# A sort in 16-bit pairs, with two self products between sort and counts, in a graph network kernel

## The reference, cut to what matters

```python
xr = jnp.einsum('nd,rde->rne', x, W_rel)            # 3 relations
msg = xr[edge_type, edge_src] + b_rel[edge_type]
agg = jax.ops.segment_sum(msg, edge_dst, num_segments=N_NODES)
xs = jnp.einsum('nd,tde->tne', x, W_self)           # 3 node types
h_self = xs[node_type, jnp.arange(N_NODES)] + b_self[node_type]
return jax.nn.relu(h_self + agg)
```

## Time and profile before

| | |
|---|---|
| median of 3 runs | 872.49 us (870.45 to 872.97) |
| the profiled execution's own time | 873.43 us |
| its span on the core | 871.7 us |
| mean granted TensorE clock | 0.965 |
| share of the span: TensorE, VectorE, ScalarE, GpSimd busy | 90%, 80%, 62%, 33% |

### The profile page before, as it was taken

The page is one execution under the profiler, slowest core; times in us unless marked ns, Lnnn a source line. Parts: engine busy times, 40 slices in busy tenths (PEclk is TensorE's granted clock), DMA queues, the critical chain, the costliest instruction groups (busy, mean ns, idle before and its releaser), DMA issues.

```text
span 871.7 us, 12030 instructions
## 1 busy us (share of the span) xinstructions
PE 785.7 (90%) x3566; PEld 600.5 (69%) x3566; DVE 698.3 (80%) x1253; ACT 542.8 (62%) x1034; POOL 284.5 (33%) x230
## 2 busy tenths in 40 slices
PE   2979799899789889988998999999999999999895
PEld 2657565477467668766777877786777867778674
DVE  7999856799966968887898788977889878997635
ACT  2298213566563422646897678877788677864646
POOL 3000387777300000016760068400863028710000
PEclk9989999999989999998999999999999999999998
DMA  5423246788472340416993199822996249942001
GB/s 118 119 69 104 72 135 191 222 255 253 144 262 95 109 132 1 130 64 169 221 228 115 36 228 225 210 91 79 230 228 158 86 126 211 233 103 69 26 6 54
DMA packets 61330, 122.12 MB, mean 140 GB/s; under 512 B 9097, under 2 KB 22699, under 8 KB 61270
## 3 DMA queue, kind: packets, MB, share of 16 engines
q0 software_dynamic: 22096, 52.18, 27.1%
q1 hardware_dynamic: 39173, 69.17, 25.2%
HBM read 105.60 MB, written 15.73 MB: 139 GB/s over the span
## 4 chain that ended last, share of the span: by engine, by line
PE 60%; DVE 22%; ACT 11%; DMA 4%; issue 3%; POOL 0%; SPq 0%; ACTq 0%; DVEq 0%; POOLq 0%
PE ps L712 12%; PE ps L1046 10%; PE ps L1030 7%; PE ps L1085 7%; PE ps L1070 6%; DVE z_parts L1962 5%; PE ps L820 4%; PE ps L965 3%; PE ps L911 3%; DVE gathered_parts L1709 2%; DVE w L1469 2%; PE ps L704 2%; ACT slot_recs L1149 2%; ACT queued L1301 2%; PE ps L849 2%
## 5 line engine op out<-in xcount | busy, mean ns | idle before, releaser
L680 POOL DMA_INDIRECT queued<-node_rows,srci x92 | 145.5, 1581 | 192.3 <-DMA node_rows<-work 152.9
L1046 PE MATMUL ps<-z_parts,onehot_dst 128*125 128x512 f32 x664 | 190.7, 399 | 2.8 <-DVE z_parts L1962 1.6
L712 PE MATMUL ps<-w,xT 128*125 128x512 f32 x660 | 169.9, 410 | 4.2 <-DVE w L1469 3.1
L1962 DVE SCALAR_TENSOR_TENSOR z_parts<-ps,z_parts 128x512 fp32r<-128x512 f32 x216 | 146.4, 689 | 27.4 <-ACT z_parts L1361 22.4
L1361 ACT ACTIVATE z_parts<-ps 128x512 fp32r<-128x512 f32 x216 | 128.1, 597 | 45.4 <-PE ps L1030 36.9
L712 PEld LDWEIGHTS ps<-w,xT 128*125 128x125 f32 x660 | 125.7, 194 | 35.7 <-issue 5.5
L1046 PEld LDWEIGHTS ps<-z_parts,onehot_dst 128*125 128x125 f32 x664 | 120.3, 186 | 42.4 <-issue 15.0
L1030 PE MATMUL ps<-x_parts,gather_lhs 128*128 x408 | 129.1, 398 | 0.5 <-DVE z_parts L1962 0.5
L1030 PEld LDWEIGHTS ps<-x_parts,gather_lhs 128*128 128x128 f32 x408 | 76.4, 188 | 19.9 <-issue 2.5
L1962 DVE SCALAR_TENSOR_TENSOR z_parts<-queued,z_parts 128x512 fp32r<-128x512 f32 x116 | 79.6, 686 | 7.2 <-ACT z_parts L1361 6.8
L674 POOL DMA_INDIRECT gathered<-rel_rows,rowi x75 | 77.8, 1038 | 22.9 <-issue 21.3
(11 more groups left out here) (285 smaller groups left out, 1125.0 us busy)
## 6 DMA issues: line engine op xcount, KB each, us to landing
w_stage<-in_weights SPq DMA_DIRECT2D x88, 256.0 KB, 3.8
onehot_dst<-onehot_rows SPq DMA_DIRECT2D x80, 250.0 KB, 5.2
onehot_rows<-onehot_dst SPq DMA_DIRECT2D x20, 250.0 KB, 2.4
gather_lhs<-edge_src_rows SPq DMA_DIRECT2D x8, 432.0 KB, 8.3
node_rows<-work SPq DMA_DIRECT2D x20, 160.0 KB, 1.9
queued<-node_rows,srci POOLq DMA_INDIRECT x116, 6.6
node_rows<-work SPq DMA_DIRECT2D x20, 90.0 KB, 2.0
rel_rows<-rel_rows_out SPq DMA_DIRECT2D x10, 160.0 KB, 1.9
```

The costliest lines, as they stand in the source:

```text
L680: gp.indirect_dma_start(Q[k % QR][:, :], None, xb_d, row, compute_op=ALU.add)\
L712: mm = pe.matmul(ps[0:R, bank, :], lt[:, a, k, n * R:(n + 1) * R], w[:, b, k, :], start=first and k == 0 and (a, b) == THREE[0], stop=last ...
L1046: mm = pe.matmul(psf[0:R, bass.ds(d, D)], S[:, j // SK % SR, j % SK, :], Z[:, g % ZR, a, :], start=False, stop=False, skip_group_check=True)
L1962: v.scalar_tensor_tensor(out=Z[:, g % ZR, LO, :], in0=of, scalar=0.0, in1=Z[:, g % ZR, HI, :].bitcast(F32), op0=ALU.max, op1=ALU.subtract) ...
```

## The change

Six edits, all in the first 150 us:

1. The sort's one-hots and products become 16-bit numbers (bf16, and f16 for the record values), laid out as `[pair of columns, value, 2]`, so that the innermost dimension has two neighbours and a step of one in every operand. TensorE reads each column at a step of two. The record values and the weights no longer share a type, so a slot column takes two matmuls, of 166 and of 249 columns, where it took one of 332.
2. The edge weight is kept as three bf16 parts in place of two. VectorE makes the first two parts' products in six of the eight groups (`VEC_W`), and the first part's in the other two; ScalarE makes the rest.
3. The count one-hots compare f16 copies of the records (`slh`, `dlh`) with an f16 pair table (`iota2`) in the same layout.
4. Two transposes of x and the split of the first weights move ahead of VectorE's rank chain, and the bias rows are loaded before the weights.
5. `w_lows(3)` and `w_highs(3)` move from the counts to the end of the sort. Two of the five node tiles of the first self product (the blocks in `SEQ` order, 1 and 2) are made before the counts, in banks 6 and 5, one ahead of the record transposes and one behind them; the other three go among the counts, a piece at each fifth tile from tile 18 on.
6. The first three groups of message one-hots are made before VectorE waits for the counts.

```diff
-VEC_W = (3, 5, 7)
+VEC_W = (0, 2, 3, 4, 6, 7)
-FIRST_FILL, FILL_STEP = 20, 3
+FIRST_FILL, FILL_STEP = 18, 5
+SEQ = (1, 2, 3, 4, 0)
+EARLY = 2
+SBANK = (6, 5, 7, 7, 7)
...
-        OHL = at(l_at, 0, "slot_low", [EP, 2, SG, P], F32R)
-        EQ = at(l_at, 10240, "slot_high", [EP, 2, SG, TE])
-        RH = [at(l_at, 16896 + 13312 * i, f"slot_recs{i}", [EP, SG, NREC, TE], F32R) for i in range(2)]
+        OHL = at(l_at, 0, "slot_low", [EP, 2, SG // 2, P, 2], BF16)
+        EQ = at(l_at, 10240, "slot_high", [EP, 2, SG // 2, TE, 2], BF16)
+        RV = [at(l_at, 16896 + 3328 * i, f"slot_values{i}", [EP, SG // 2, 2, TE, 2], F16) for i in range(2)]
+        RWT = [at(l_at, 23552 + 4992 * i, f"slot_weights{i}", [EP, SG // 2, 3, TE, 2], BF16) for i in range(2)]
...
+            pe.wait_ge(x_in, 16 * len(ROWS))
+            for n in range(2):
+                transposes(n, B[0:R, n, :])
             pe.wait_ge(tot_made, 1)
...
+                if g == 0:
+                    zeros(7)
                 for c in range(SG):
-                    mm = pe.matmul(ps[:, 7, 0:NREC * TE], OHL[:, g % 2, c, :],
-                                   RH[g % 2][:, c, :, :].rearrange("p a t -> p (a t)"),
-                                   start=g == 0 and c == 0, stop=g == NSG - 1 and c == SG - 1)
+                    pe.matmul(ps[:, 7, 0:2 * TE], OHL[:, g % 2, c // 2, :, c % 2], RV[g % 2][:, c // 2, :, :, c % 2],
+                              start=False, stop=False, skip_group_check=True)
+                    mm = pe.matmul(ps[:, 7, 2 * TE:5 * TE], OHL[:, g % 2, c // 2, :, c % 2],
+                                   RWT[g % 2][:, c // 2, :, :, c % 2], start=False, stop=False, skip_group_check=True)
...
+            pe.wait_ge(words_made, 1)
+            for j in range(KT):
+                fill(j)
+            pe.wait_ge(rec_made, 1)
+            pe.transpose(ps[0:TF, 7, 0:P], slf[:, 0:TF], ident[:, :])
+            pe.transpose(ps[0:TF, 7, P:2 * P], wt[:, 0:TF], ident[:, :]).then_inc(rec_tr, 1)
+            pe.wait_ge(yb_out, NREL * NT)
+            for b in range(3):
+                zeros(b)
+            for j in range(KT, 2 * KT):
+                fill(j)
+            pe.wait_ge(typ_out, 1)
+            for b in (3, 4):
+                zeros(b)
+            for b in (6, 5):
+                pe.wait_ge(self_out, SBANK.index(b) + 1)
+                zeros(b)
...
-                for a in ((LO,) if g in VEC_W else (HI, LO)):
+                for a in ((2,) if g in VEC_W else (1, 2)):
                     for c in range(SG):
...
+            self_first(0)
             act.wait_ge(rec_tr, 1)
             nc.scalar.copy(tr_sl[:, :], ps[0:TF, 7, 0:P])
             nc.scalar.copy(tr_w[:, HI, :], ps[0:TF, 7, P:2 * P]).then_inc(rec_rows, 1)
-            act.wait_ge(y_done, NREL * NT)
-            w_highs(3)
...
+            v.wait_ge(rows_hi, 1)
+            v.tensor_tensor(RWL, RW, RWH.bitcast(F32), ALU.subtract).then_inc(rows_split, 1)
+            for n in range(2):
+                tr_low(n, XT, n, n + 1)
+            w_lows(0)
             v.scalar_tensor_tensor(out=loc[:, :, :], in0=blk[:, :, :], scalar=-float(R), in1=ids[:, :, :],
...
+                for a in ((0, 1) if g in VEC_W else (0,)):
+                    v.tensor_tensor(RWT[g % 2][:, :, a, :, :], EQ[:, g % 2, :, :, :],
+                                    per_slot(wbits[:, a, :], g, TE), ALU.mult)
                 for i in range(2):
-                    ins = v.tensor_tensor(RH[g % 2][:, :, i, :], EQ[:, g % 2, :, :],
-                                          val[:, i, c].unsqueeze(2).broadcast_to([EP, SG, TE]), ALU.mult)
+                    ins = v.tensor_tensor(RV[g % 2][:, :, i, :, :], EQ[:, g % 2, :, :, :],
+                                          per_slot(val[:, i, :], g, TE), ALU.mult)
...
+            w_lows(3)
             v.wait_ge(so_used, NSG)
...
+                for to, of in ((SS, slh), (SD, dlh)):
+                    ins = v.tensor_tensor(to[:, g % 2, :, :, :], local_ids(CG), per_tile(of, g * CG, CG), ALU.is_equal)
                 ins.then_inc(cnt_made, 1)
...
+            for g in range(1, SR):
+                onehots(g)
             v.wait_ge(c_done, 1)
```

More of the change, by code:

```diff
@@ L173, in build @@
         bk = early("bk", [EP, EC])
-        val = early("record_values", [EP, 2, EC])
-        wparts = early("weight_parts", [EP, 2, EC], F32R)
+        val = early("record_values", [EP, 2, EC], F16)
+        wparts = early("weight_parts", [EP, 3, EC])
+        wbits = early("weight_parts_b", [EP, 3, EC], BF16)
         slot = early("slot", [EP, EC])
         ti = early("ti", [EP, 2, EC], I32)
-        lohi = early("lohi", [EP, 2, EC])
+        lohi = early("lohi", [EP, 2, EC], F16)
         tri = early("tri", [EP, P])
@@ L753, in _ @@
             pe.matmul(ps[:, 7, NB:2 * NB], ones[:, :], run[:, :, EC - 1], start=True, stop=True).then_inc(pre_made, 1)
-            pe.wait_ge(x_in, 16 * len(ROWS))
-            for n in range(NT):
+            for n in range(2, NT):
                 transposes(n, B[0:R, n, :])
@@ L824, in fill @@
                     mm.then_inc(self_done, 1)
+            pe.wait_ge(words_made, 1)
[15 more added lines that the diff above has]
+                zeros(b)
             def first_fill(t):
                 j, late = divmod(t - FIRST_FILL, FILL_STEP)
[L828 to L832, removed]
+                if not late and 0 <= j < (NT - EARLY) * KT:
+                    fill(EARLY * KT + j)
             for g in range(NCF):
@@ L1129, in _ @@
             act.wait_ge(edges_in, 64)
-            nc.scalar.copy(wparts[:, HI, :], e_w[:, :]).then_inc(wp_hi, 1)
-            for n in range(NT):
-                tr_high(n, XT, n, n + 1)
+            nc.scalar.copy(wbits[:, 0, :], e_w[:, :]).then_inc(wp_hi, 1)
+            act.wait_ge(wp_hi, 1)
+            nc.scalar.copy(wparts[:, 0, :], wbits[:, 0, :]).then_inc(wp_hi, 1)
             act.wait_ge(rows_in, 16 * 7)
             nc.scalar.copy(RWH, RW).then_inc(rows_hi, 1)
+            for n in range(2):
+                tr_high(n, XT, n, n + 1)
             w_highs(0)
+            act.wait_ge(wp_low, 1)
+            nc.scalar.copy(wbits[:, 1, :], wparts[:, 2, :]).then_inc(wp_hi, 1)
+            act.wait_ge(wp_hi, 3)
+            nc.scalar.copy(wparts[:, 1, :], wbits[:, 1, :]).then_inc(wp_hi, 1)
+            for n in range(2, NT):
+                tr_high(n, XT, n, n + 1)
+            act.wait_ge(wp_hi, 4)
+            act.wait_ge(wp_low, 2)
             def rel_copy(r, n):
@@ L1188, in m_high @@
                 nc.scalar.copy(M[:, t % MR, HI, :], G[place(t)][:, :]).then_inc(m_hi, 1)
-            for n in range(3):
-                self_first(n)
+            for i in range(1, 3):
+                self_first(i)
             for t in range(AHEAD):
                 m_high(t)
-            for n in range(3, NT):
-                self_first(n)
+            for i in range(3, NT):
+                self_first(i)
             act.wait_ge(c_done, 1)
@@ L1474, in w_lows @@
                     w_low(j, k)
+            v.wait_ge(rows_hi, 1)
+            v.tensor_tensor(RWL, RW, RWH.bitcast(F32), ALU.subtract).then_inc(rows_split, 1)
+            for n in range(2):
+                tr_low(n, XT, n, n + 1)
+            w_lows(0)
+            v.scalar_tensor_tensor(out=loc[:, :, :], in0=blk[:, :, :], scalar=-float(R), in1=ids[:, :, :],
+                                   op0=ALU.mult, op1=ALU.add)
+            link(v.tensor_copy(typ[:, :], e_typ[:, :]))
+            link(v.scalar_tensor_tensor(out=val[:, 0, :], in0=typ[:, :], scalar=float(NT), in1=blk[:, 0, :],
+                                        op0=ALU.mult, op1=ALU.add))
+            link(v.scalar_tensor_tensor(out=val[:, 0, :], in0=val[:, 0, :], scalar=float(P), in1=loc[:, 0, :],
+                                        op0=ALU.mult, op1=ALU.add))
+            v.tensor_scalar(val[:, 0, :], val[:, 0, :], 1.0, None, ALU.add)
+            v.tensor_scalar(val[:, 1, :], loc[:, 1, :], 1.0, None, ALU.add)
+            v.wait_ge(wp_hi, 1)
+            v.tensor_tensor(wparts[:, 2, :], e_w[:, :], wbits[:, 0, :], ALU.subtract).then_inc(wp_low, 1)
             v.wait_ge(pre_made, 1)
@@ L1487, in _ @@
                                         in1=run[:, 0:NB - 1, EC - 1], op0=ALU.add, op1=ALU.subtract))
-            for n in range(NT):
+            for n in range(2, NT):
                 tr_low(n, XT, n, n + 1)
-            v.wait_ge(rows_hi, 1)
-            v.tensor_tensor(RWL, RW, RWH.bitcast(F32), ALU.subtract).then_inc(rows_split, 1)
-            w_lows(0)
+            v.wait_ge(wp_hi, 3)
+            v.wait_ge(wp_low, 1)
+            v.tensor_tensor(wparts[:, 2, :], wparts[:, 2, :], wbits[:, 1, :], ALU.subtract).then_inc(wp_low, 1)
             link(v.tensor_tensor(run[:, :, :], run[:, :, :], adj[0:EP, :].unsqueeze(2).broadcast_to([EP, NB, EC]),
```

117 lines of the change are left out of this document (54 added, 63 removed).

## The result

| | before | forecast | after |
|---|---|---|---|
| median (20 runs each) | 873.37 us (870.01 to 885.43) | 866.4 by the median of 872.49 | 869.70 us (864.76 to 873.53) |
| first sort matmul | 48.90 | 46.95 | 46.16 |
| T8, last sort group leaves TensorE | 90.6 | 87.7 | 85.3 |
| first count | 99.5 | 103.1 | 100.6 |
| first rest tile | 121.7 | 117.4 | 115.0 |

The ratio leaves out the old kernel's two slow executions, 884.20 and 885.43 us. It is 0.996 [0.9941, 0.9979]: the kernel is faster by 0.4%, where the forecast had 0.7%. At the copy of the counts the lead is 6.65 us, half a microsecond more than the forecast; the medians are 3.7 apart. So some 3 us are given back later, and the 6.65 are not made of the parts that the prediction named.

A forecast was written before the change was run, and what follows sets the result against it. TensorE, busy 90% of the span, was taken as the bound wherever its data is in time. The sum -2.9 (sort) - 3.3 (sort to count copy) = -6.2 us, -6.1 against the median, gave 866.4 us, range 862.5 to 872.8.

The forecast's parts named there:

- VectorE's rate: VectorE's two-operand 16-bit instructions: half the cost per value, giving 820, 586 and 1,353 ns.
- Both 16-bit rivals: Sort: 16-bit pairs bring VectorE no rate (7%, 877 us); twice the matmuls at full price (6%, 875 us).
- the second: Sort on TensorE: twice the matmuls at full price, 3.22 us a group, 875 us; loss above 142 ns a matmul; 6%.
- Ranks: nothing: Rank chain before the sort: VectorE does nearly the same instructions, so 0, within 0.5 us either way.
- Start of the sort: First sort matmul: 46.95 us in place of 48.90, a gain of 1.9 us.
- A sort group: Sort on TensorE: twenty shorter matmuls take 2.1 us a group in place of 1.61, +0.5 each.
- From T8 to the copy: From the last sort group's end to the copy of the counts: 49.4 us in place of 52.7, -3.3.
- the fourth rival: Full counts: five counts cost 5 x 0.215 us and the piece nothing, or the other way; -2.3, 864 us; 15%.
- the third rival: Counts: five between pieces leave TensorE less busy; open pieces or a clock fall cost up to 3.6 us, 870; 17%.
- The gathers: GpSimd's first gather, recorded at 16.61 us, falls to about 1 us; those behind it gain 0.
- Messages: 0: Message stage: two one-hots of 0.68 us leave VectorE's queue where TensorE waits for none; gain 0.
- the fifth rival: Messages: the copy comes early but a gather or weight load then ends last, 872 us; 5%.

The follow-up runs named there:

- the first trace: Profile of the unaltered changed kernel from the result, beside the old kernel; median 869.70 us, ratio 0.996.
- the third run: The changed kernel unaltered, run again as the mark for three variants on a quick chip, against the old kernel; 869.67 us, ratio 0.9947.
- the third group: Four follow-up runs on a chip as quick as the result's: the changed kernel and three variants, beside the old kernel at 872.45 us.
- `pairs_only`: Edits 1 to 3 alone, splits and message one-hots back in their old places, against the old kernel; ratio 0.9893.
- `start_back`: Changed kernel without edit 4, transposes of x and first weights' split behind the ranks again, against the old kernel; ratio 0.9819.
- `start_step3`: Changed kernel with pieces at every third tile from 18 and edit 4 undone, against the old kernel; 872.14 us, ratio 0.9991.
- `step3`: Changed kernel with pieces at every third tile in place of every fifth, none among the rest tiles, against the old kernel; 871.26 us, ratio 0.9993.

## Why the prediction was right, and where it was not

- **VectorE's rate**: right within 4 ns (820, 585, 1,349 against 820, 586, 1,353), and shown to be what the sort's gain rests on. Both 16-bit rivals fall; the second would have turned to a loss at 144 ns a matmul by its own sum, not at 142.
- **Ranks: nothing**: right within the scatter; the cast of `lohi` is 0.7 us earlier in the trace (38.9 against 39.6), and 0.0 to 0.8 earlier in the three traces without edit 4.
- **Start of the sort**: 46.16 against 46.95. Almost all of it is the rank chain's 0.7. TensorE's idle stretch moved from 44 to 35, as foreseen; its price, a tile of 4.56 in place of 3.06, lay beside VectorE's work.
- **A sort group**: 1.83 us in the mean against 2.1; over eight groups this is 2.2 us. From the start of a group's tile to the next group it is 3.4 against 3.31, over seven tiles 0.6 the other way. With the 0.8 of the start this makes the 2.4 by which T8 was early. The 0.8 for the small transposes and ScalarE's twenty products is there (5.97 in place of 5.2, once). A pair takes 190 ns, less than the line of 0.47 ns a column and 5 ns gives without any margin (205). The Trainium skill (TensorE: Matmul & The Clock Gate, "LDWEIGHTS") gives P / 1.2 ns for a load of P columns, by which an estimate for 128 columns is 107 ns; the 166-column matmul starts 80 ns before the next (46.24 - 46.16), and a pair with its two loads takes 190, so the measurement decides, also for columns at a step of two.
- **From T8 to the copy**: this is the step that failed. Forecast 49.4, measured 51.3, and the gain isn't the two self tiles', to which the sum gave it: without edit 5 it is 50.6, so that what shortens the old 52.7 is edit 3's cheaper one-hots (edit 6 comes too late for it). Up to the first rest tile it holds (29.7 us in both), though partly by luck: five counts with a piece cost 1.05, below the forecast's 1.38, as the fourth rival said, and the fall of the clock at 104 to 108 (1.5 us) and a longer wait on bank 7 took it back, the first as the third rival said. The rest tiles were forecast at 17.1 + 4 x 0.54 = 19.3 and took 21.4. I had split the 2.31 us of three tiles and a piece by the busy 1.77 of the tiles; but where two kinds of matmuls overlap, busy time is no price. A row with tiles alone would have given most of it. The old trace has one before the end:

```profile
139.03 3.06 PE L849 MATMUL ps<-onehot_dst_rest,onehot_src_rest 128*128 128x128 bf16 x25
142.37 0.74 PE L849 MATMUL ps<-onehot_dst_rest,onehot_src_rest 128*128 128x128 bf16 x5 [0.28 <-issue]
```

Five tiles in 3.34 are 0.67 each; with the 0.31 that this leaves for a piece the stage would have been put at 20.6.
- **The gathers**: right for the first (1.05 us at 95.95 in place of 16.61).
- **Messages: 0**: no run shows a step of the change that costs anything there; but the lead of 6.65 becomes 3.7 in the medians. The prediction named a lead gone by 240 us as a sign that it is wrong: the first trace has 6.8 at 235, the third run 0.4. That run is what the fifth rival described, a copy that comes early and a gather that then ends last. In executions at like clock (0.968 or more) the changed kernel has a mean of 867.3 us (16 of 32 runs on two chips; 866.8 in 5 of 12 on the third group's alone), the old one 871.8 (19 of 29 there). Of the changed kernel's 32 runs 6 are at 0.960 or below, of the old one's 29 none. This suggests that one to two of the microseconds given back are a clock that falls more often. Why it does, and where the rest goes, stays open: the traces show the falls at places where TensorE waits in both kernels, and late gathers in one execution.

The time was forecast at 866.4 and is 869.7, inside the range; the own range of the forecast, 864.5 to 868.5, missed it by 1.2.

## What to carry to other kernels

Price an instruction in a mixed stream by the distance between starts with it and without it, never by its busy time: what looked like 0.54 us was 0.1, and an edit built on it gained nothing at the copy. Long matmuls put between many short ones were nearly free here; the same matmuls made in the open cost their whole length. For the two-operand instructions here, one float32 operand cost the whole 16-bit rate: look at each operand, not at the output. A version for the next step would be the pieces spread from the first count on with no self tile in the open; it was not run.

## What the runs showed of the hardware

- Two of the three chips of the experiments run both kernels 3 to 4% slower (908 us in place of 872 for the old one, 897 in place of 870 for the changed one). Up to 116 us they keep pace within 1.5 us; from 110 to 240 us TensorE, VectorE and ScalarE are idle together for 10 to 22 us in all, up to 6.6 at a time, while GpSimd's gathers go on. In the traces from the two quick chips it is 1.0 at most.
- The same order of work keeps the clock or loses it: with 2.5 us of idle TensorE ahead of the sort, the clock fell in `pairs_only` and `start_back` (first group's pairs 0.35 us apart) and stayed at 1.00 in `start_step3` (0.19).
- The time of a run goes with its mean granted clock: 864.8 us at 0.971, 873.5 at 0.956, correlation -0.83 over twenty runs of one kernel.
- The small matmuls of the rest tiles take the same time at either clock (2.77 us for twenty at 1.00, 2.67 at 0.50, `step3`).
